# Holding back SyncE's loads behind the first query-weight block in a cross-attention kernel on one Trainium2 core

## The reference

```python
memory_proj = jnp.einsum('bme,de->bmd', memory, W_mem)
scores = jnp.einsum('bnd,bmd->bnm', hidden_states, memory_proj) / jnp.sqrt(jnp.float32(D))
attn = jax.nn.softmax(scores, axis=-1)
memory_context = jnp.einsum('bnm,bmd->bnd', attn, memory_proj)
gate_input = jnp.concatenate([hidden_states, memory_context], axis=-1)
gate = jax.nn.sigmoid(jnp.einsum('bnf,df->bnd', gate_input, W_gate) + b_gate)
fused = hidden_states + gate * memory_context
return _rmsnorm(fused, norm_w)
```

## Time and profile before

| what | value |
|---|---|
| median of 3 runs | 116.98 us (116.87 to 117.26) |
| profiled execution | 116.94 us, of which the span is 115.1 us |
| PE busy | 108.6 us, 94% of the span |
| PE weight loads | 90.3 us, 78% |
| DVE, ACT, POOL busy | 71.3, 68.5, 28.0 us |
| DMA | 22.64 MB, mean 197 GB/s |

### The profile page before, as it was taken

How to read it: one execution, slowest core, us unless ns; L and a number is a source line. 1 busy time by engine, 2 the same in 40 slices (tenths; PEclk the granted TensorE clock), 3 DMA queues, 4 the chain that set the end, 5 groups by cost and what they waited for, 6 DMA issues and landing times.

```text
span 115.1 us, 1536 instructions
## 1 busy us (share of the span) xinstructions
PE 108.6 (94%) x504; PEld 90.3 (78%) x504; DVE 71.3 (62%) x105; ACT 68.5 (60%) x114; POOL 28.0 (24%) x30
## 2 busy tenths in 40 slices
PE   7999999999999999999999999999999999999900
PEld 7878888888888888888888888888888888888900
DVE  0299989987999456000449759999373021366891
ACT  4298979999652756420958577766364402047561
POOL 1000000000000009890394000670059000036640
PEclk9999999999999999999999999999999999999995
DMA  3999998769999999940000487899952400003604
GB/s 72 306 383 328 283 384 314 258 232 276 277 321 239 224 347 297 394 182 1 0 0 3 182 285 169 298 272 243 262 224 75 182 0 0 6 0 134 228 2 182
DMA packets 13975, 22.64 MB, mean 197 GB/s; under 512 B 1552, under 2 KB 6416, under 8 KB 13968
## 3 DMA queue, kind: packets, MB, share of 16 engines
q1 hardware_dynamic: 12960, 21.40, 58.5%
q10 hardware_dynamic: 1008, 1.15, 4.0%
HBM read 16.25 MB, written 6.29 MB: 196 GB/s over the span
## 4 chain that ended last, share of the span: by engine, by line
PE 89%; DMA 4%; ACT 1%; issue 1%; DVE 1%; POOLq 1%; POOL 0%; ACTq 0%
PE wide L860 19%; PE wide L879 19%; PE wide L823 19%; PE wide L775 10%; PE wide L890 9%; PE wide L907 8%; PE wide L839 5%; DMA ring<-xT 4%; ACT squares L474 1%; POOLq L29 1%; POOL rstd L382 0%; ACT res L565 0%; DVE gate L655 0%; DVE xT_hi L683 0%; ACT gate L554 0%
## 5 line engine op out<-in xcount | busy, mean ns | idle before, releaser
L391 POOL TENSOR_TENSOR res<-gate,vecs 128x512 f32<-128x512 f32 x7 | 8.5, 1210 | 34.4 <-DVE gate L644 34.4
L377 POOL TENSOR_TENSOR ctxT_lo<-ring,ctxT_hi 128x512 fp32r<-128x512 f32 x4 | 5.6, 1420 | 42.7 <-ACT ctxT_hi L414 42.7
L621 DVE TENSOR_TENSOR wgT_lo<-wide,wgT_hi 128x512 fp32r<-128x512 f32 x4 | 2.7, 688 | 19.5 <-ACT wgT_hi L461 19.5
L823 PE MATMUL wide<-ctxT_hi,qT_hi 128*128 128x512 f32 x32 | 12.4, 389 | 0.0
L823 PE MATMUL wide<-ctxT_lo,qT_hi 128*128 128x512 f32 x32 | 12.4, 389 | 0.0
L823 PE MATMUL wide<-ctxT_hi,qT_lo 128*128 128x512 f32 x32 | 12.4, 389 | 0.0
L426 ACT ACTIVATE probs<-wide,neg_max 128x1024 f32<-128x1024 f32 x8 | 8.9, 1108 | 3.5 <-DVE neg_max L589 3.3
L589 DVE TENSOR_REDUCE neg_max<-wide 128x1 f32<-128x1024 f32 x8 | 9.7, 1212 | 1.8 <-PE wide L823 1.7
L432 ACT ACTIVATE probs<-probs,inv_sum 128x1024 f32<-128x1024 f32 x8 | 9.2, 1148 | 0.7 <-DVE inv_sum L594 0.7
L461 ACT ACTIVATE wgT_hi<-wide 128x512 fp32r<-128x512 f32 x4 | 2.3, 597 | 10.6 <-PE wide L860 10.6
L879 PE MATMUL wide<-wgT_hi,xT_hi 128*128 128x512 f32 x32 | 8.6, 389 | 0.0
(11 more groups left out here) (90 smaller groups left out, 247.5 us busy)
## 6 DMA issues: line engine op xcount, KB each, us to landing
ring<-ctxT SPq DMA_DIRECT2D x8, 256.0 KB, 4.9
ring<-w_gateT SPq DMA_DIRECT2D x8, 256.0 KB, 5.5
ring<-ctxN SPq DMA_DIRECT2D x8, 256.0 KB, 6.8
xr<-x_rows SPq DMA_DIRECT2D x8, 256.0 KB, 5.0
out<-res SPq DMA_DIRECT2D x7, 256.0 KB, 2.0
ring<-xT SPq DMA_DIRECT2D x6, 256.0 KB, 6.6
passage<-spare SPq DMA_DIRECT2D x3, 512.0 KB, 3.8
passage<-ring SPq DMA_DIRECT2D x3, 512.0 KB, 3.0
```

The source lines that it names most:

```text
L377: nc.gpsimd.tensor_tensor(lo, slot(i), hi.bitcast(f32), ALU.subtract).then_inc(lo_pool, 1)
L391: nc.gpsimd.tensor_tensor(res[:, j % 2], gate[:, j % 2, 1:], gain, ALU.mult)\
L823: last = nc.tensor.matmul(sums("scores", j, h), qT_s[left][:, c, rows], ctxT_s[right][:, c, cols], start=(c == 0 and (left, right) == (HI, ...
```

## The change

SyncE issues blocks 0 and 2, then waits until block 0 has landed (all 16 increments of its semaphore), and only then goes on with blocks 4, 5, 6 and the rest. ScalarE still issues blocks 1 and 3 at once. Nothing else is altered: `FIRST_LOADS` is 4, `load` skips the blocks of `BY_ACT`.

```diff
@@ -164,6 +164,7 @@
 
         FIRST_X = index_of["xT", 0, 0]
         act_hi = [i for i in range(NB) if i != FIRST_X]
+        FIRST_LOADS = index_of["xT", 0, 1] + 1
         dve_lo = list(range(FIRST_ON_POOL))
         pool_lo = list(range(FIRST_ON_POOL, NB))
 
@@ -321,7 +322,10 @@
                     sp.dma_start(placed[j][r * QUAD:(r + 1) * QUAD].rearrange("j (q f) -> j q f", q=NQ),
                                  quarters[r]).then_inc(landed[j], 16)
 
-            load(*range(26))
+            load(*range(FIRST_LOADS))
+
+            sp.wait_ge(loaded[index_of["wm", 0, 0]], 16)
+            load(*range(FIRST_LOADS, 26))
             send(0)
             send(1)
             fetch(0)
```

## The result

The changed kernel took 119.07 us (median of 6 executions, 118.24 to 120.2) against 116.93 us before (6 executions, 116.46 to 117.26): ratio 1.0171, 95% interval 1.014 to 1.0202. It is slower by 1.7%. Every ratio in this document leaves out executions over 1.5% above the fastest of the same kernel, here the one of 120.2 us. The profiled execution is the fastest of the six: 118.24 us with a span of 116.4 us, 1.3 us more than before. The median's loss is 119.07 - 116.93 = 2.1 us, so about 0.8 us of it are not in the trace that is read here.

The account below looks back on a forecast made before the run. It took PE, unbroken from 5.64 to 108.15 us, as the bound, with tight slack at `qT_lo` behind block 9. Sum: 116.94 us plus a 0.10 us stall, 117.04 us; range 116.4 to 117.7 us.

Parts of the forecast that it names:

- The tight place: Low part of the first query chunk: block 9, splits, `qT_lo`, then PE's weight load at 11.62 us; slack 0.07 us.
- a sign of being wrong: PE waiting at another place, above all at the second group of query matmuls on blocks 4 to 7.
- Blocks 5 to 9 are bound by bandwidth in both kernels: Loads behind block 4: block 9 lands 3.07 us after it, at 9.67 us, giving PE a 0.10 us stall.
- the 2.9 us I took: Block 4's time from issue to landing behind the wait, so it lands at 6.6 us, 0.16 us later than before.
- the slower rival: Block 4 meets latency the queue no longer hides; 117.6 us if it takes 3.5 us, 118.5 if 4.4; chance 0.27.
- my row: Profile row of block 0's load, 2.9 us to landing, used as the price of block 4's fresh load.
- the sum drawn from it: Total of 116.94 us if block 4 took 2.3 us by the skill page's fixed cost and bandwidth.
- the 0.2 us that I held to be the most: Front of the kernel: block 1 earlier by at most 0.2 us from 0.06 MB fewer bytes beside it; costed at nothing.
- the floor given: PE's start limited by its warm-up, about 0.35 us earlier than before, in the faster rival.
- The faster rival: Early stretch runs better with fewer transfers in flight; block 9 some 0.4 us earlier, 116.5 us; chance 0.26.
- the far case: Range's upper end: the slower rival with block 4 at 3.5 us, block 9 landing at 10.3 us, 117.6 us.

Follow-up runs that it names:

- full-load run: Changed kernel with three full 256 KB loads issued by SP between block 2 and the wait: 119.7 us, ratio 1.022 to the kernel before.
- the longer hold: Changed kernel, but SP waits for block 1 in place of block 0: 119.0 us, ratio 1.0197 to the kernel before.
- without splits: Changed kernel, but ACT and DVE start their splits only when block 9 has landed: 123.75 us, one execution.
- the small loads in the silence: Changed kernel with four 16 KB loads issued by SP between block 2 and the wait: 119.32 us, ratio 1.0214 to the kernel before.
- the wait without hold: Changed kernel, but SP waits on a semaphore already raised at 0.9 us: 116.78 us, ratio 0.9993 to the kernel before.
- the one that held from block 6 on: Changed kernel, but SP issues blocks 4 and 5 at once and holds block 6 and later: median 118.46 us, ratio 1.0085 from the six lowest of ten.
- the kernel before without splits: Kernel before, but ACT and DVE start their splits only when block 9 has landed: 123.43 us, one execution.
- the merged one without hold: Kernel before with blocks 5 and 6 as one 512 KB load and blocks 8 and 9 as one: 117.36 us, ratio 1.0027.

## Why the prediction was wrong

**The tight place** was right. The chain runs through block 9, both splits and `qT_lo` as worked out. Behind block 9 it took 13.01 - 11.01 = 2.0 us to the end of `qT_lo`, against 2.05 us foreseen, and behind that the pieces are those of before, moved by 1.33 us at the gate matmuls. One wait on this way was not foreseen: PE also waited 0.6 and 0.4 us in the second group of query matmuls, for the parts of the late blocks. The prediction named a wait there as a sign of being wrong. It adds nothing to the sum, since PE had to wait at the scores in any case.

**The step that failed** is "Blocks 5 to 9 are bound by bandwidth in both kernels", with its 3.07 us from block 4 to block 9. That interval was measured behind full queues. Behind the hold it was 5.2 us. PE's load of `qT_lo` came 13.05 - 11.62 = 1.43 us later, in place of 0.10 us. The full-load run shows that the interval goes back to 3.1 us when the queues are kept full by three more loads. I had the sign of it in the rows: from 2.5 to 5 us, when the queues were filling, the kernel before moved 98 to 292 GB/s, and I took this for the start of the program alone.

**Block 4** landed 2.2 us after its issue, less than the 2.9 us I took; 2.1 us with the longer hold and without splits. The fresh load itself was cheaper than priced, and the slower rival was wrong in its mechanism: not block 4's latency but the rate of what followed. The number that I drew from the Trainium skill's fixed cost, an estimated 2.3 us (DMA: Bandwidth & Descriptors, "Anatomy of one DMA", fitted there for another issue path), was nearer than my row; the sum drawn from it, 116.94 us, was further off than mine.

**Block 1** came 0.8 us earlier, four times the 0.2 us that I held to be the most. The 0.06 MB of the held blocks bounded the bytes, not the delay. In the layout of before it landed at 4.2 to 4.4 us in the kernels in which SP was silent from 1.6 to 2.2 us or longer, at 4.8 us with the small loads in the silence, and at 5.0 us in the kernel before, in the one with the wait without hold and in the one that held from block 6 on. That silence is not the whole of it: block 1 landed at 4.5 us, in one profiled execution each, in the kernel before without splits and in the merged one without hold, where SP went on issuing. PE started 0.47 us earlier, close to the floor given. That it would all be lost at `qT_lo` was right.

**The faster rival** got its early block 1 and not its early block 9: from 7 to 10 us the rate was 294 GB/s, not more.

**The range** ended at 117.7 us since it took 3.5 us for block 4 as the far case, while the interval behind it had no bound of its own.

**Open.** Why the transfers behind a hold run slowly for 1.5 to 5 us is not shown, nor how much must be queued ahead of them so that they don't: it isn't the splits alone, the number of loads or the issues, and the layout has a part in some stretches. Why the profiled execution of the change is 0.8 us faster than the median of all six is not shown either.

## What to carry to other kernels

Don't price what stands behind a new wait by an interval taken from full queues: the first loads behind a hold may move at a half or a third of that rate, though they are all issued, so look in the trace for a stretch in which the queues were filling and take its rate. Where one landing sets the end of a chain with 0.07 us of slack, a hold of the queue in front of it can cost its own length and more, even when other transfers seem to cover it. Before paying for an earlier start, follow the chain to the next place with little slack: here two stood behind it, at 11.6 and at 85.9 us.

## What the runs showed of the hardware

- Loads of 256 KB behind a hold moved at 126 GB/s (5.5 to 7.0 us) and 294 GB/s (7 to 10 us), and without any compute beside them at 225 and 266 GB/s; the same loads joining full queues moved at 386 GB/s. The kernel without the hold moved 400 and 346 GB/s in these two stretches.
- At 226 GB/s over 4.5 us the engines still counted as busy for 0.91 of the time: the DMA share doesn't tell a full rate from a slow one.
- With blocks in one piece in HBM, the rate at 2.5 to 3.0 us after the start was 334 in place of 98 GB/s, with rows of 2 KB in both. Block 9 landed at 9.5 us in both.
- Loads that SP issued at 1.64 and 2.10 us went with a block 1, on ACT's queue and issued 0.9 us before, that landed 0.8 us later, though only 0.06 MB of them had moved by then. In the kernel without splits, with the same issues, block 1 landed at 4.5 us, so the issues alone don't set it.
